# A decoder's two layers: another start of the program, and re-ordered queues behind it

## The reference

```python
qkv = einsum('bse,ef->bsf', norm(x), qkv_kernel) + qkv_bias     # layer 0, 16 heads of 8
attn = softmax(q @ k^T * scale + causal)                         # per head, 64 x 64
x = x + attn @ v
x = x + cross_attention_0(norm(x), ctx)                          # one head
x = x + experts_0(norm(x))     # 8 experts, top 2 by gate, and one shared: silu(W1) * W3, then W2
x = x + gelu(state_scan(norm(x))) normalised, scaled, cleaned of nan and inf   # layer 1
x = x + cross_attention_1(norm(x), ctx, mask)                    # 8 heads of 64
x = x + experts_1(norm(x))     # 8 experts; each takes its 128 best tokens
```

## Time and profile before

| | us |
|---|---|
| median of 3 runs | 290.12 (289.47 to 291.55) |
| the profiled execution's own time | 287.52 |
| its span, first to last instruction | 285.8 |
| TensorE busy | 250.7 |
| VectorE busy | 205.5 |
| ScalarE busy | 147.9 |
| GpSimd busy | 71.0 |
| mean granted TensorE clock | 0.958 |

### The profile page before, as it was taken

How to read it: one execution, slowest core, us unless ns; L and a number is a source line. 1 busy time by engine, 2 the same in 40 slices (tenths; PEclk the granted TensorE clock), 3 DMA queues, 4 the chain that set the end, 5 groups by cost and what they waited for, 6 DMA issues and landing times.

```text
span 285.8 us, 5223 instructions
## 1 busy us (share of the span) xinstructions
PE 250.7 (88%) x1783; PEld 171.2 (60%) x1788; DVE 205.5 (72%) x738; ACT 147.9 (52%) x307; POOL 71.0 (25%) x124
## 2 busy tenths in 40 slices
PE   0789699999998998999994678789997999999993
PEld 0345488786664574666672343565885657667783
DVE  4735788788875856758337967985867488889964
ACT  1366455445446469675773126236555754444541
POOL 5264795000000234543674010014420000000000
PEclk9999899999999999999999558899999999999999
DMA  5469960013803000000000000000000000000002
GB/s 148 106 175 217 252 173 1 2 28 107 236 0 73 2 1 0 1 3 0 0 2 1 0 1 0 2 2 2 2 3 1 2 0 0 3 0 0 2 0 75
DMA packets 22039, 11.63 MB, mean 41 GB/s; under 512 B 11016, under 2 KB 21005, under 8 KB 22013
## 3 DMA queue, kind: packets, MB, share of 16 engines
q1 hardware_dynamic: 21117, 11.01, 14.5%
q0 software_dynamic: 80, 0.20, 0.7%
q10 hardware_dynamic: 816, 0.10, 0.2%
HBM read 8.68 MB, written 2.62 MB: 40 GB/s over the span
## 4 chain that ended last, share of the span: by engine, by line
PE 67%; DVE 13%; DMA 6%; ACT 5%; issue 5%; POOL 2%; SPq 1%; DVEq 0%; POOLq 0%; ACTq 0%
PE bank L895 10%; PE bank L883 9%; PE bank L748 5%; PE bank L653 4%; PE bank L632 4%; PE bank L754 4%; PE bank L773 3%; PE bank L868 3%; PE bank L540 2%; PE bank L639 2%; DMA v_scratch<-QKVT 2%; PE bank L575 2%; POOL X L496 2%; DVE XN L1529 2%; DVE stats L1489 1%
## 5 line engine op out<-in xcount | busy, mean ns | idle before, releaser
L496 POOL TENSOR_TENSOR X<-X,att 128x128 f32<-128x128 f32 x72 | 30.6, 458 | 76.7 <-ACT att L1277 76.5
L883 PE MATMUL bank<-XT,Wb 128*128 128x512 f32 x64 | 30.3, 602 | 0.7 <-ACT XT L1138 0.7
L895 PE MATMUL bank<-Wb,att 128*128 128x128 f32 x256 | 30.7, 277 | 0.0
L895 PEld LDWEIGHTS bank<-Wb,att 128*128 128x128 f32 x256 | 29.7, 192 | 1.4 <-issue 1.4
L1277 ACT ACTIVATE att<-bank,comb 128x128 f32<-128x128 f32 x72 | 20.2, 377 | 9.3 <-PE bank L773 9.3
L1317 ACT ACTIVATE att<-bank 128x512 f32<-128x512 f32 x32 | 18.8, 600 | 9.6 <-PE bank L883 9.6
L1702 DVE SCALAR_TENSOR_TENSOR att<-bank,cols,att 128x512 f32<-128x512 f32 x18 | 13.5, 750 | 12.0 <-ACT att L1266 5.9
L773 PEld LDWEIGHTS bank<-W2a,att 128*128 128x128 f32 x144 | 18.3, 192 | 5.7 <-issue 5.5
L1840 DVE SCALAR_TENSOR_TENSOR X<-big,rt,X 128x128 f32<-128x128 f32 x64 | 17.7, 348 | 3.9 <-ACT big L1325 3.7
L1325 ACT ACTIVATE big<-bank 128x512 f32<-128x512 f32 x16 | 9.6, 598 | 19.5 <-PE bank L895 19.5
L773 PE MATMUL bank<-W2a,att 128*128 128x128 f32 x144 | 19.2, 278 | 0.0
(11 more groups left out here) (232 smaller groups left out, 521.1 us busy)
## 6 DMA issues: line engine op xcount, KB each, us to landing
Wb<-in_L_ffn_W SPq DMA_DIRECT2D x1, 1024.0 KB, 5.4
Wb<-in_L_ffn_W SPq DMA_DIRECT2D x8, 128.0 KB, 5.1
X<-in_x SPq DMA_DIRECT2D x2, 256.0 KB, 3.1
k_scratch<-QKVT SPq DMA_DIRECT2D x1, 512.0 KB, 2.6
q_scratch<-QKVT SPq DMA_DIRECT2D x1, 512.0 KB, 3.0
Wb<-k_scratch SPq DMA_DIRECT2D x1, 512.0 KB, 4.9
V<-q_scratch SPq DMA_DIRECT2D x1, 512.0 KB, 5.4
v_scratch<-QKVT SPq DMA_DIRECT2D x1, 512.0 KB, 6.3
```

Source lines behind the costliest of these rows:

```text
L496: nc.gpsimd.tensor_tensor(X[:, h * HT + t, :], X[:, h * HT + t, :], part0[:, i % 2, t, :], ALU.add).then_inc(f_acc, 1)
L883: mm(bank[i % 4][:, :], W1b[:, e, f * P:(f + 1) * P], XT[:, half(h)], start=True, stop=True).then_inc(m_up, 1)
L895: last = mm(bank[4 + h][:, t * P:(t + 1) * P], hid[:, e % 2, f, tile], W2b[:, e, f, :], start=(f == 0), stop=(f == F1 - 1))
```

## The change

- **Products of ones.** A memset of VectorE writes ones to the first 128 columns of XT (`warm`). TensorE waits for it and makes 16 products of 128 by 128 by 128 from it into bank 7, transposes the vectors, and makes 8 more.
- **Transposes first.** Both halves of XN are transposed ahead of the six projection products, and these now run keys, keys, queries, queries, values, values. ScalarE copies both halves of XT first, then in the products' order.
- **One root.** The first norm takes the moments of both halves, one root over 8 columns, and then writes both halves.
- **Value store.** SyncE issues it ahead of the load of the queries.
- **Value copy first.** GpSimd copies the values ahead of all eight `widen_keys`, not behind the second.
- **Orders.** In the written-out lists behind sequence 8 many calls change places with neighbours, on TensorE, ScalarE, VectorE and GpSimd. No call is added or left out there. Of TensorE's list the diff below shows two places: the state scan's second half and the last norm.

```diff
+        warm = XT[:, 0:P]
...
             load(1, st_k, Wb[:, 0:N], ld_kh)
+            store(2, v_copied, st_v)
             load(0, st_q, V2[:, :, :].rearrange("p c s -> p (c s)"), ld_qh)
-            store(2, v_copied, st_v)
             load(2, st_v, Wb[:, N:2 * N], ld_vh)
...
-            widen_keys(0)
-            widen_keys(1)
             pool.wait_ge(ld_vh, 16)
             nc.gpsimd.tensor_copy(VD[:, :, 0, :].rearrange("p n (c t) -> p n c t", t=GT), VH).then_inc(vd_pool, 1)
             pool.wait_ge(vd_pool, 1)
-            for a in range(2, NPAIR):
+            for a in range(NPAIR):
                 widen_keys(a)
...
-            add_bias(0)
             weigh_probs(0)
             weigh_probs(1)
+            add_bias(0)
             weigh_probs(2)
-            add_bias(1)
             weigh_probs(3)
             weigh_probs(4)
+            add_bias(1)
...
+            def fill(n):
+                for _ in range(n):
+                    mm(bank[7][:, 0:P], warm, warm, start=True, stop=True)
...
+            pe.wait_ge(c_warm, 1)
+            fill(16)
             pe.wait_ge(c_ident, 1)
             pe.wait_ge(ld_vecs, 128)
             nc.tensor.transpose(bank[4][:, 0:31], vecs[:, :], ident[0:31, 0:31]).then_inc(prep_psum, 1)
+            fill(8)
+            for h in range(2):
+                transpose_xn(0, h, h)
             pe.wait_ge(c_wp, 1)
             pe.wait_ge(prep_act, 1)
-            for h in range(2):
-                transpose_xn(0, h, h)
-                pe.wait_ge(xt_ready[h], 1)
-                for i, s in enumerate((1, 0, 2)):
+            for i, s in enumerate((1, 0, 2)):
+                for h in range(2):
+                    if i == 0:
+                        pe.wait_ge(xt_ready[h], 1)
                     mm(bank[2 + 3 * h + i][:, :], Wp[:, s, :], XT[:, half(h)], start=True, stop=True
                        ).then_inc(p_psum[h], 1)
...
             transpose_xn(3, 1, 6)
+            inject(1)
             keys_values1(13)
-            inject(1)
             widen(1, 0)
             widen(1, 1)
             widen(1, 2)
+            keys_values1(14)
             widen(1, 3)
-            keys_values1(14)
             widen(1, 4)
             widen(1, 5)
             read_out(1)
+            keys_values1(15)
             transpose_xn(4, 0, 0)
-            keys_values1(15)
...
+            transpose_xn(5, 0, 6)
             project_out(6)
             project_out(7)
-            transpose_xn(5, 0, 6)
             up1(0, 0, 0)
+            up1(0, 1, 0)
+            down1(0, 0)
+            transpose_xn(5, 1, 6)
             route(0)
-            up1(0, 1, 0)
-            transpose_xn(5, 1, 6)
-            down1(0, 0)
             route(1)
...
             AF(cols[:, :], bank[4][:, 0:31], ACT.Copy).then_inc(prep_act, 1)
             copy_xt(0, 0, 0)
+            copy_xt(0, 1, 1)
...
             AF(head_rows(1, 0), by_head(2), ACT.Identity, bias=cols[:, 1:2]).then_inc(k_copied, 1)
-            copy_xt(0, 1, 1)
+            act.wait_ge(p_psum[1], 1)
+            AF(head_rows(1, 1), by_head(5), ACT.Identity, bias=cols[:, 1:2]).then_inc(k_copied, 1)
...
+            def root_tiles(h):
+                return slice(0, NT) if h is None else tiles(h)
...
+            V.memset(warm, 1.0).then_inc(c_warm, 1)
             for h in range(2):
                 dve.wait_ge(ld_x[h], 16)
-                layernorm(0, h)
+                ln_moments(0, h)
+            root(None)
+            for h in range(2):
+                ln_apply(0, h)
```

More of the change, by code:

```diff
@@ L946, in _ @@
             weigh_values(8)
-            scores(12)
             transpose_probs(10)
             weigh_values(9)
+            scores(12)
             scores(13)
             scores(14)
+            scores(15)
             transpose_probs(11)
             weigh_values(10)
-            scores(15)
             transpose_probs(12)
@@ L957, in _ @@
             keys_values1(4)
+            weigh_values(11)
+            transpose_probs(13)
+            transpose_probs(14)
             keys_values1(5)
-            transpose_probs(13)
-            weigh_values(11)
+            keys_values1(6)
+            transpose_xn(1, 0, 7)
             weigh_values(12)
-            keys_values1(6)
-            transpose_probs(14)
-            transpose_xn(1, 0, 7)
             cross0_q(0)
@@ L983, in _ @@
             up0_third(0, 0)
-            outputs_by_token(1)
             up0_third(0, 1)
             up0_first(0, 2)
+            outputs_by_token(1)
             down0(0, 0)
             up0_third(0, 2)
+            up0_third(0, 3)
+            down0(0, 1)
+            up0_third(0, 4)
             gate_transpose(0)
@@ L1015, in _ @@
             up0_first(1, 0)
+            down0(0, 8)
+            up0_third(1, 0)
+            up0_third(1, 1)
             up0_first(1, 1)
[L1017 to L1020, removed]
+            up0_first(1, 2)
+            down0(1, 0)
+            up0_first(1, 3)
             up0_third(1, 2)
-            down0(1, 0)
-            up0_first(1, 2)
+            up0_third(1, 3)
+            down0(1, 1)
+            up0_first(1, 4)
             gate_transpose(1)
[L1025 to L1029, removed]
+            up0_third(1, 4)
             down0(1, 2)
-            up0_third(1, 4)
+            transpose_xn(3, 0, 7)
+            down0(1, 3)
             up0_third(1, 5)
-            transpose_xn(3, 0, 7)
-            up0_first(1, 6)
-            down0(1, 3)
             inject(0)
@@ L1038, in _ @@
             widen(0, 0)
+            up0_first(1, 5)
+            up0_first(1, 6)
+            widen(0, 1)
             up0_third(1, 6)
-            widen(0, 1)
-            up0_third(1, 7)
[L1042 to L1047, removed]
+            widen(0, 2)
+            up0_first(1, 7)
+            widen(0, 3)
+            down0(1, 5)
+            down0(1, 6)
+            widen(0, 4)
+            up0_third(1, 7)
             widen(0, 5)
@@ L1365, in _ @@
             silu(0, 1)
+            silu(0, 2)
             weigh0(0, 0)
-            silu(0, 2)
             silu(0, 3)
             weigh0(0, 1)
+            silu(0, 4)
             copy_xt(1, 1, 6)
-            silu(0, 4)
+            weigh0(0, 2)
             cross0_q(1)
-            weigh0(0, 2)
+            weigh0(0, 3)
             silu(0, 5)
@@ L1391, in _ @@
             weigh0(1, 0)
-            gate_copy(1)
             silu(1, 2)
             silu(1, 3)
+            gate_copy(1)
+            weigh0(1, 1)
             silu(1, 4)
-            weigh0(1, 1)
+            copy_xt(3, 0, 7)
             weigh0(1, 2)
-            copy_xt(3, 0, 7)
+            weigh0(1, 3)
             silu(1, 5)
+            weigh0(1, 4)
             silu(1, 6)
-            weigh0(1, 3)
-            weigh0(1, 4)
+            silu(1, 7)
             weigh0(1, 5)
-            silu(1, 7)
             weigh0(1, 6)
@@ L1493, in moments @@
                 then(last)
+            def root_tiles(h):
+                return slice(0, NT) if h is None else tiles(h)
             def root_guess(h):
-                r, var, y, t = (rs[:, i, tiles(h)] for i in range(4))
-                then(V.tensor_scalar(var, mv[:, tiles(h), 1], EPS, None, ALU.add))
+                r, var, y, t = (rs[:, i, root_tiles(h)] for i in range(4))
+                then(V.tensor_scalar(var, mv[:, root_tiles(h), 1], EPS, None, ALU.add))
                 then(V.tensor_scalar(r.bitcast(int32), var.bitcast(int32), -0.5, float(0x5f3759df), ALU.mult, ALU.add))
@@ L1903, in _ @@
             gate0(0, 6)
+            gate0(0, 7)
             cross0_add(1)
@@ L1929, in _ @@
             state(0, 2)
+            gate0(1, 5)
+            state(0, 3)
             gate0(1, 6)
-            state(0, 3)
             state(0, 4)
```

128 lines of the change are left out of this document (61 added, 67 removed).

## The result

| | before | after |
|---|---|---|
| median of 20 runs each, us | 289.16 (287.26 to 291.55) | 294.92 (291.19 to 296.69) |
| ratio of the runs | | 1.017, 95% interval 1.014 to 1.020 |
| the profiled execution, us | 287.52 | 291.19 |
| its span; mean granted clock | 285.8; 0.958 | 289.3; 0.943 |

The predicted 286.1 was wrong in sign. Medians here are of all runs, while the ratios leave out runs more than 1.5% above their kernel's fastest, so the two can differ. The profiled execution of after is its fastest run; it shows 3.67 of the 5.8 us.

The account below looks back on a forecast made before the run. TensorE was taken to carry most of the chain, except a relay of loads, projections and stores in the first 34 us. Terms -2.35 - 2.2 + 0.5 = -4.0 us took the median from 290.12 to 286.1, range 283.0 to 289.3.

Parts of the forecast that it names:

- The start: Load to fourth softmax: scores at 25.7 us instead of 28.03 (2.35 us), plus 2.2 of waits; fourth softmax 4.5 us sooner.
- VectorE's 2.2 us of waits: Before the fourth softmax: three VectorE waits for TensorE (1.08, 0.64, 0.49 us), on value transposes and work queued behind, all go.
- no later than it could have: SyncE's queue: the query load, issued behind the value store, leaves when the query store has landed, at 18.5 us.
- The ones: Kernel start: sixteen products of ones end near 7 us, before the vectors land at 7.61, and are free; six projections take 0.87 each.
- GpSimd: Widenings behind the value copy: done at 44.9 us, not binding the ninth scores, with 0.4 us left.
- The orders: Lists after 60 us: most swaps cost nothing where TensorE is full; together +0.5 us, between -2 and +3.
- Two of the signs: Signs of a wrong forecast: TensorE less busy in 60 to 150 us; scan's read-out later than 4 us ahead of its present place.
- The rival of losing orders: Attention starts move by 4.5 us, but the orders add 2.5 to 3 by waits in 70 to 110 us: 288.8; chance 0.17.
- The rival of the clock: Scan's end: the clock stays at 1.2 GHz into the second softmax; slower than before, 293 with 7 us of work; chance 0.04.
- The scan: State scan's second half: product 13 moved between injection and first widening; the widening of 162.50 us starts about 0.5 later.

Follow-up runs that it names:

- e1: The changed kernel's new start with every list behind sequence 8 in the old order, against before: 286.57 us, ratio 0.987.
- e12: e7 with SyncE issuing the query load ahead of the value store, as in the kernel before: 284.69 us, ratio to before 0.981.
- e11: e1 without the 24 products of ones: 285.58 us, ratio to before 0.987.
- B: The part of the re-ordered lists covering experts 0 and the first half of the state scan; e6 has it alone on the new start: 293.41 us.
- e6: e1 with the new order only in experts 0 and the first half of the scan: 293.41 us, ratio to before 1.009.
- e8: The changed kernel with identity products in two of TensorE's waits (6 and 22): 288.44 us, ratio to before 0.993.
- e4: e1 with the new orders only from the scan's second half on: 287.47 us, ratio to before 0.990.
- e5: e1 with the new order only from sequence 8 to the gate of half 0: 287.09 us, ratio to before 0.992.
- e2: The kernel before, old start, with only the re-ordered lists: 298.10 us, ratio to before 1.029.
- e14: e6 with 14 identity products in three of TensorE's waits in experts 0: 288.77 us, ratio to before 0.987.
- e10: e6 with two places put back, around cross attention 0's second half and gate_second(0) behind gate0(0, 0): 296.38 us, ratio to before 1.022.
- e7: e1 with identity products in three of TensorE's waits (5, 22 and 7): 281.97 us, ratio to before 0.974.

## Why the prediction was wrong

**The start: right.** Stores, transposes, scores and the fourth softmax came within 0.4 us of their forecasts; the key load left 0.6 late (17.00 for 16.4), and landed at 21.4 all the same. All of VectorE's 2.2 us of waits went, as forecast. The worth is less sure: e1 wins 3.1 us by medians and 3.9 by its ratio, and the forecast 4.5 lies inside the interval. In e1's profile the query load stays 7.4 us (18.71 to 26.1), where after has 6.2 and before 5.4, and the clock falls at 36.9 us once more. The query load behind the value store was taken as "no later than it could have"; its landing is later, as e12, with the load first, shows with 5.3 us.

**The ones: right in mechanism, wrong in worth.** They were forecast to end near 7 us and ended at 7.8. They raise the clock and take 2.0 us off the projections; the total does not show it (e11).

**GpSimd: right.** Its last widening ends at 45.1 us (41.84 and 3.22), ahead of the ninth scores.

**The orders: the step that failed.** The prediction wrote: "Most swaps sit in stretches where TensorE is full, and I cost those at nothing", and took them at +0.5, between -2 and +3. They cost 8.4 us, 6.8 of them in B. Two of the signs written down for this came: TensorE is busy 83.8 us in 60 to 150, before 86.3, and the scan's read-out starts at 172.20, before at 170.25. Two things were wrong in the step. First, a full TensorE was taken for room. Its products also cover other engines' chains, and which product stands behind which call decides whether they do; the earlier trace rows show 2.2 us of idle in 20, and I read them as 2.2 to be won or doubled. The old list left 1.4 us of waits between copy 3 and the scan's second half, the new one 4.0 (e6). I had not laid one chain (cross attention's values, then add and norm, 5.3 us) against the products behind it (3.8). Second, each wait was priced at its own length, and the clock was left out: in e6's profile 2.5 us more of waits come with 5.1 of slower products, in after's 3.3 with 1.0. How much of the 8.4 us is clock in most runs stays open; with most of it held, e8 is still 6.5 above e7.

**The rival of losing orders (0.17) had the waits** and sized them at 2.5 to 3 us, near the 2.5 of e6; it left out the clock too. Its 288.8 should by its own terms read 288.1 to 288.6.

**The rival of the clock had the right mechanism and 0.04.** It named the scan's end; there the clock did stay low in after, to 181.2 us, 7.7 later than in before. That the order there did it is not shown: e4 has the same one, and its clock rose at 173.2. That its price of 293 is 2 us from the 294.92 is luck, as most of the loss lies in B. It was tied to one place, from 4.0 us of work on. The profiles show dips from 79 (after), 88 (e5), 93 (e2), 119 (e6) and 125 us (e14) as well; the ones of after and e6 follow on waits of 0.5 to 1.7 us. A mechanism that can act at every wait needed a chance for each of them.

**The scan: undersized.** Product 13 ahead of the first widening cost about what was written (widening at 164.62 for 162.50, of which 1.67 is copy 7's own lateness: 0.45). Product 15 ahead of the transposes was not priced: 1.7 us (read-out to transposes 3.57 us in e4 and after, 1.87 in before).

**What stays open.** Why much the same waits are followed by a dip of 3.4 us in one profile and of 10.2 in another; and e10. Over 112 runs of the changed kernels (one of 510 us left out), the runs of one kernel get shorter by 1.9 us for each 0.01 more of mean clock (correlation -0.83), so most of the scatter goes with the clock.

## What to carry to other kernels

Before a call is moved in a list, take the chain that the call serves or blocks and add up the products that stand behind its start: if the cover is less than the chain, the difference is a wait, however full the engine looks. Price a wait of TensorE at its length and at what the clock may take behind it, and where a wait can't go, put idle products in it. Undo reorderings as a whole, or lay out each queue anew; swaps put back singly moved the wait here, both times.

## What the runs showed of the hardware

- Filling three waits of TensorE, 34 products of 128 by 128, was worth 4.6 us of 287 by medians, 3.6 by ratios (e1 to e7); filling two in the changed kernel, 6.5 of 295 (after to e8). Time at 1.2 GHz does not cost half of itself: 0.01 of mean clock is 5.8 us at the lower level in a run of 290, and goes with 1.9 more, not 2.9.
- The dips last from 3.4 to 23.9 us, and they come in the middle of a kernel whose TensorE is busy 88% of the time: in e6 waits of 1.08, 0.37, 1.65 and 0.69 us within 10 us stand ahead of a dip of 10.2. The Trainium skill, "TensorE: Matmul & The Clock Gate", section "A second HAM failure mode: psum-queue depth-cycling", tells of a kernel in which frequent short idle times between groups of products made the clock swing between its two levels. The traces agree in that dips follow on short waits, here for other engines and not for PSUM banks (the 1.08, 0.37, 1.65 and 0.69 us above).
- The profile page's row of the clock can't be read at the very start. Of e11 it prints 9 from the first slice, but the weight loads of the six projections come 0.85 us apart up to 15 us and 0.43 apart behind it; that is, the clock rose only there.
